# Keys and queries of every head in both row halves of the array, with odd heads scored in the upper half

## The reference

```python
x = x + attn_a(layernorm(x))   # 16 heads of 16 features, 1024 queries and 1024 keys
x = x + ffn(layernorm(x))      # ternary weights, exact gelu
x = x + attn_b(layernorm(x))   # attends over the heads of one token
x = x + ffn(layernorm(x))

def attn_a(x):                 # lora_linear: x W^T + b + 0.5 (x B^T) A^T
    q, k, v = split(lora_linear(x, Wq, ..)), split(lora_linear(x, Wk, ..)), split(lora_linear(x, Wv, ..))
    scores = einsum('bhqd,bhkd->bhqk', q, k) * SCALE
    out = einsum('bhqk,bhkd->bhqd', softmax(scores), v)
    return lora_linear(out, Wo, ..)
```

## Time and profile before

| | us |
|---|---|
| median of 3 runs | 355.96 |
| lowest and highest of them | 355.44, 357.6 |
| the profiled execution, its own time | 356.57 |
| its span from the first to the last instruction | 354.8 |
| busy in the span: PE, DVE, ACT, POOL | 328.0, 281.7, 264.0, 128.7 |
| units 2 to 5, between the first multiplications by V of neighbouring units | 20.3 each |

### The profile page before, as it was taken

One profiled execution on the slowest core, in us unless ns is written; L12 is line 12 of the kernel. 1 busy time (PEld: TensorE's weight loads), 2 busy tenths in 40 slices (PEclk: granted clock), 3 DMA queues, 4 the chain that ended last, 5 costly groups with the idle time before them and its releaser, 6 DMA issues.

```text
span 354.8 us, 5514 instructions
## 1 busy us (share of the span) xinstructions
PE 328.0 (92%) x1909; PEld 147.0 (41%) x1909; DVE 281.7 (79%) x471; ACT 264.0 (74%) x465; POOL 128.7 (36%) x133
## 2 busy tenths in 40 slices
PE   7999787999989999999999999999998957979796
PEld 2653442222222222222222234438745723647685
DVE  6456999799989999999999543517959998899774
ACT  1575114799989999999999977996479442577694
POOL 5042019999100000000005000400499976995030
PEclk9999997899999999999999999999999996999899
DMA  7936962353340000000000000000000000000011
GB/s 225 309 62 116 155 165 48 66 127 69 59 91 0 3 0 3 0 1 2 0 3 1 3 0 1 2 0 2 0 3 0 1 0 2 0 0 2 1 61 59
DMA packets 14814, 14.57 MB, mean 41 GB/s; under 512 B 4995, under 2 KB 13126, under 8 KB 14598
## 3 DMA queue, kind: packets, MB, share of 16 engines
q1 hardware_dynamic: 12358, 12.09, 14.9%
q10 hardware_dynamic: 2176, 1.64, 1.5%
q0 software_dynamic: 256, 0.52, 0.9%
HBM read 5.78 MB, written 1.05 MB: 19 GB/s over the span
## 4 chain that ended last, share of the span: by engine, by line
PE 63%; DVE 12%; SPq 10%; ACT 7%; issue 4%; DMA 2%; POOL 2%; ACTq 0%; DVEq 0%; POOLq 0%
PE ps L1417 14%; PE ps L1403 12%; SPq L535 8%; PE ps L1557 6%; PE ps L1545 6%; PE ps L1380 5%; PE ps L1332 4%; DVE mx L1095 3%; PE ps L1530 3%; PE ps L1589 2%; PE ps L1362 2%; DMA pack<-m_rows 1%; ACT ps L929 1%; PE ps L1300 1%; DVE s_wide L1202 1%
## 5 line engine op out<-in xcount | busy, mean ns | idle before, releaser
L888 ACT ACTIVATE pbuf<-ps,exp_scale 128x512 f32<-128x512 f32 x256 | 156.5, 693 | 13.7 <-PE ps L1403 10.9
L1095 DVE TENSOR_REDUCE mx<-ps 128x1 f32<-128x1024 f32 x128 | 150.4, 1219 | 11.1 <-PE ps L1380 8.1
L1403 PE MATMUL ps<-pack 64*128 64x512 f16 x256 | 87.9, 387 | 3.4 <-ACT pbuf L888 1.3
L1417 PE MATMUL ps<-pbuf,v_slot 128*32 128x512 f32 x512 | 68.8, 611 | 1.3 <-ACT parts L873 1.3
L1403 PEld LDWEIGHTS ps<-pack 64*128 64x128 f16 x256 | 23.1, 94 | 88.1 <-ACT pbuf L888 61.7
L1380 PE MATMUL ps<-pack 64*128 64x512 f16 x128 | 48.8, 385 | 4.8 <-DVE mx L1095 4.5
L1380 PE MATMUL ps<-parts,pack 64*128 64x512 f16 x128 | 49.9, 394 | 0.0
L750 POOL TENSOR_TENSOR pbuf<-wT 128x1024 f32<-128x1024 f32 (+3 forms) x32 | 48.2, 1534 | 3.5 <-ACT wT L958 3.4
L705 POOL COPY v_slot<-v_sb 128x512 f32<-128x512 f32 x8 | 4.9, 614 | 114.5 <-PE ps L1417 93.0
L681 POOL TENSOR_TENSOR rstd<-rstd,minus_half 128x2 f32<-128x2 f32 x16 | 11.4, 715 | 72.9 <-DVE rstd L1014 72.9
L1189 DVE SCALAR_TENSOR_TENSOR pack<-ps,g_unit,pack 128x512 f16<-128x512 f32 (+1 forms) x40 | 24.6, 639 | 14.1 <-ACT pack L941 14.1
(11 more groups left out here) (145 smaller groups left out, 392.7 us busy)
## 6 DMA issues: line engine op xcount, KB each, us to landing
w_nat<-in_L_ffn_w_dram SPq DMA_DIRECT2D x2, 1024.0 KB, 7.0
pack<-pack SPq DMA_DIRECT2D x3, 512.0 KB, 4.9
pack<-pbuf SPq DMA_DIRECT2D x20, 64.0 KB, 3.1
x_res<-in_L_attn_a_x_dram SPq DMA_DIRECT2D x4, 256.0 KB, 4.0
pack<-parts SPq DMA_DIRECT2D x16, 64.0 KB, 2.3
pack<-parts SPq DMA_DIRECT2D x32, 32.0 KB, 2.0
out_dram<-x_res SPq DMA_DIRECT2D x4, 256.0 KB, 2.1
w_nat<-in_L_attn_b_Wqkv_dram ACTq DMA_DIRECT2D x1, 768.0 KB, 6.7
```

Source lines behind the costliest of these rows:

```text
L888: act.activation(pbuf[:, c % 2, j, :], ps[:, b, :], ACT.Exp, scale=exp_scale[:, 0:1]).then_inc(drained[b], 1)
L1095: dve.tensor_reduce(mx[:, par, k:k + 1], ps[:, b:b + 2, :].rearrange("p b k -> p (b k)"), AX_X, ALU.max) \
L1403: pe.matmul(ps[:, b, :], k_group[0:ROWS, at, j, P * c:P * c + P].rearrange("p g t -> p (g t)"), q_rows[0:ROWS, at, qh, j, :].rearrange("p ...
L1417: ins = pe.matmul(ps[32 * j:32 * j + 32, PV_BANK, :], v_slot[:, qh, c, j, :], pbuf[:, c % 2, j, :], start=(c == 0), stop=(c == TT - 1))
```

## The change

The upper row half now holds all keys, not the far half alone, and they lie in `k_rows` and no longer in `k_far`. For group 0, one DMA more copies the near keys of its four heads up. For groups 1 to 3 the copy of the keys is 512 KB instead of 256 KB. The shift is written by two DMAs, one into each row half, and whoever waits for a shift waits for both. `score_tile` takes keys and queries of heads 1 and 3 of a group from the upper row half; heads 0 and 2 stay in the lower. The max pass reads its far keys from `k_rows`.

```diff
@@ far_keys
-            spread(eng, k_far[ROWS:2 * ROWS, h, :], K_, h, slice(HALF, T), done)
+            spread(eng, k_rows[ROWS:2 * ROWS, h, HALF:T], K_, h, slice(HALF, T), done)
@@ SP, group 0
             sp.dma_start(q_rows[ROWS:2 * ROWS, 0, 1, :, :], q_rows[0:ROWS, 0, 1, :, :]).then_inc(second_half_repeated, 16)
+            for j in range(G):
+                sp.wait_ge(head_packed[j], 32)
+            sp.dma_start(k_rows[ROWS:2 * ROWS, 0:G, 0:HALF], k_rows[0:ROWS, 0:G, 0:HALF]).then_inc(far_keys_packed, 16)
@@ SP, whole_group
-                sp.dma_start(k_far[ROWS:2 * ROWS, G * g:G * g + G, :], k_rows[0:ROWS, G * g:G * g + G, HALF:T]) \
-                    .then_inc(group_repeated[g], 16)
+                sp.dma_start(k_rows[ROWS:2 * ROWS, G * g:G * g + G, :].rearrange("p h t -> p (h t)"),
+                             k_rows[0:ROWS, G * g:G * g + G, :].rearrange("p h t -> p (h t)")).then_inc(group_repeated[g], 16)
@@ SP, land_shift
-                sp.dma_start(q_rows[SHIFT_ROWS[g // 2], g, qh, :, :].rearrange("o h t -> o (h t)"),
-                             m_rows[0:TWO * n, :]).then_inc(shift_landed, 16)
+                rows = SHIFT_ROWS[g // 2]
+                for r in (0, ROWS):
+                    sp.dma_start(q_rows[rows.start + r:rows.stop + r:rows.step, g, qh, :, :].rearrange("o h t -> o (h t)"),
+                                 m_rows[0:TWO * n, :]).then_inc(shift_landed, 16)
@@ ACT, ahead of the first exponential
-            for done in (far_keys_packed, second_half_packed):
-                act.wait_ge(done, 16 * G)
+            act.wait_ge(far_keys_packed, 16 * G + 16)
+            act.wait_ge(second_half_packed, 16 * G)
@@ PE, max_tile
-                for n, keys in ((0, k_group[0:ROWS, at, j, 0:HALF]), (1, far_group[ROWS:2 * ROWS, at, j, :])):
+                for n, keys in ((0, k_group[0:ROWS, at, j, 0:HALF]), (1, k_group[ROWS:2 * ROWS, at, j, HALF:T])):
@@ PE, score_tile
-                pe.matmul(ps[:, b, :], k_group[0:ROWS, at, j, P * c:P * c + P].rearrange("p g t -> p (g t)"),
-                          q_rows[0:ROWS, at, qh, j, :].rearrange("p g t -> p (g t)"), start=True, stop=True) \
+                r = slice(ROWS * (j % 2), ROWS * (j % 2) + ROWS)
+                pe.matmul(ps[:, b, :], k_group[r, at, j, P * c:P * c + P].rearrange("p g t -> p (g t)"),
+                          q_rows[r, at, qh, j, :].rearrange("p g t -> p (g t)"), start=True, stop=True) \
                     .then_inc(filled[b], 1)
@@ PE, ahead of unit 0 and of each next unit
-                    pe.wait_ge(far_keys_packed, 16 * G)
-                    pe.wait_ge(shift_landed, 16)
+                    pe.wait_ge(far_keys_packed, 16 * G + 16)
+                    pe.wait_ge(shift_landed, 32)
...
-                            pe.wait_ge(shift_landed, (u + 2) * 16)
+                            pe.wait_ge(shift_landed, (u + 2) * 32)
```

More of the change, by code:

```diff
@@ L313, in build @@
         last_halves = parts[:, 2048:8192].bitcast(F16).rearrange("p (m a t) -> p m a t", m=2, a=TWO + 1)
-        k_far = parts[:, 8192:16384].bitcast(F16).rearrange("p (h t) -> p h t", h=H)
         o_un = parts[:, 0:8192].bitcast(F32).rearrange("p (g t) -> p g t", g=NG)
@@ L320, in build @@
         k_group = pack[:, 0:16384].bitcast(F16).rearrange("p (g j t) -> p g j t", g=NG, j=G)
-        far_group = parts[:, 8192:16384].bitcast(F16).rearrange("p (g j t) -> p g j t", g=NG, j=G)
         g_hi = pack[:, 0:16384].bitcast(F16).rearrange("p (k f t) -> p k f t", k=KEPT, f=FC)
```

## The result

The changed kernel takes 359.31 us, the median of 22 runs (355.55 to 362.08), against 355.88 us for the kernel before in 22 runs beside it (353.6 to 357.95). The ratio is 1.0076, interval [1.0052, 1.01]: 0.8% slower, inside the 1% that the forecast calls no change. Ratios here are taken from the fast executions alone (four of the changed kernel's 22, at 361.5 us and over, count as slow), so they need not be the quotients of the medians, here 1.0096. The forecast was 357.2 us, so the time lies 2.1 us above it, 0.6 us above the forecast's own range of 356 to 358.7, and inside the wide range of 354.5 to 360.2. The profiled execution took 359.75 us, 3.2 us more than that of before; its span is 357.9 us.

A forecast was written before the change was run, and what follows sets the result against it. ACT alone bounds the steady units, PE the tail. Profiled 356.57 + 2.7 (unit 2's shift delay) - 1.5 (tail) = 357.8, by the median 357.2 us; own range 356 to 358.7, wide range 354.5 to 360.2.

The forecast's parts named there:

- a rival that I gave 0.14: Units 1 and 2: PE's longer gaps make the clock fall; at unit 2 this costs 2.8 us, giving 360.0; chance 0.14.
- Steady units, 0: Units 2 to 5: upper-half scores save PE 0.4 us per four steps, but PE waits for ACT: 0.
- Tail, -1.5: Tail, 210 to 232 us: one score pair in each of seven groups overlaps, 0.22 us each: 1.5 us less.
- gains nothing: Tail: other work takes the place of the scores, so no gain there, 358.7 us; chance 0.12.
- Group 0's near keys, 0: Extra 256 KB copy ahead of group 1: hidden by SP's 5.0 us wait for the first shift, 0; otherwise 2.0.
- The delay of unit 2's shift, +2.7: SP's queue: two second shift writes, 0.7 each, plus 1.3 for group 3's larger key copy: landing 2.7 us later.
- one unknown: Second bias load's 2.04 us on SP, amid group 2's copies: may grow or shrink by 1.3 us; taken as no change.
- group 2's extra transfer does not count a second time: At unit 2's shift: 24 small DMAs follow group 2's copy in 16 us and their issue sets the pace; nothing added.
- Unit 1's loss lies inside unit 2's: ACT's loss of about 1.9 us at unit 1 is contained in unit 2's 2.7 us delay, not added.
- a sign of being wrong: In the changed profile, a clock below 1.00 behind 83 or 105 us would speak against the forecast.
- hidden or half as large: Shift delay on SP: faster 8 KB-row copies or a shorter bias load shrink it, about 355.2 us; chance 0.15.
- PE was not the bound: Rival for units 0 to 5: PE is the bound, so some 48 rounds shrink, 19 us in all, 336; chance 0.03.

The follow-up runs named there:

- the second set: The changed kernel, unaltered, run again beside versions with idle matmuls in its gaps: 361.36 us, 1.0142 of the kernel before.

## Why the prediction came out as it did

**The change stayed under 1% in the first set, as forecast, and the mechanism was right; two terms were mis-sized, and a rival that I gave 0.14 happened in some executions.** The time missed the forecast's own range by 0.6 us, and the wide range held it because it was drawn out to the rivals. By the steps:

*Steady units, 0.* Right: 102.63 us for five units before and after, and PE's waits for ACT 15 us longer.

*Tail, -1.5.* Measured -1.2. Groups of three fell to 0.60 us and pairs to 0.39, as the step says; by the distance between starts the seven groups gained 0.21, 0.21, 0.19, 0.14, 0.22, 0.04 and 0.21 us, so most of the missing 0.3 is one pair that still took 0.56 us. The rival "gains nothing" is out.

*Group 0's near keys, 0.* Right: the first shift goes out at 54.88 (54.99 before).

*The delay of unit 2's shift, +2.7.* Measured +3.74. The two second writes cost 0.72 and 0.71 of SP's time, against 0.7 each. First issue to last landing grew from 4.39 to 5.90, 1.5, against 1.3 for the transfer alone. And the term that I entered at zero was there: the bulk copies and bias loads of group 2 took 5.23 us of SP's time instead of 4.17, **+1.06**, since the first bias load held SP 1.17 us longer. These sum to 4.0; small gains elsewhere on SP take back 0.26. This is the step that failed: "one unknown", taken at no change where the profile after shows it near its slow end of 1.3. With it falls the sentence that group 2's extra transfer does not count a second time: SP was held 1.06 us longer behind it, and the 24 small copies, whose issue is the pace, began that much later. I named a cause that fits, a queue that 256 KB more would keep full, and the key copy cut in two restored the 0.69; the reason to take the middle was only that two causes were possible. At unit 1 the forecast landing, 82.7, was met at 82.74, but the bytes sit elsewhere than I put them: 1.06 us as time of SP ahead of the issue and 0.3 behind it, not 1.3 behind it. The Trainium skill, page "DMA: Bandwidth & Descriptors", section "Anatomy of one DMA — SWDGE (gpsimd) path", gives its fit for DMAs of the gpsimd path, and these are issued by SP; an estimate by its bytes over 436 GB/s would have made the delay 2.0 us. The landings measured here don't agree with that: behind the larger key copy the query copy lands 6.2 us after its issue (median), 4.9 before, 1.3 us more for 256 KB where the estimate is 0.6.

*Unit 1's loss lies inside unit 2's.* Right in every execution read of the changed kernel: unit 2's start was set by the landing, also where ACT had lost 3.45 us at unit 1. The 0.46 us that the prediction gives as PE's wait at unit 1 is that of a weight load; PE's matmuls have no wait there before the change, and at unit 2 the weight load's wait is 1.70 us beside PE's 1.21.

*The clock.* The forecast had it at 1.00 behind both gaps, as behind the wait of 1.21 us at unit 2 before the change:

```profile
102.00:104.00 2.00, 1.71 (x13) 0.46 (x13) 1.20 (x2) 1.20 (x3) 0.00 (x0) 1.00 0.00 0
```

It fell behind unit 1's in the first profile, which the prediction had named as a sign of being wrong, and behind unit 2's in the second. At clock 1.00 the measured terms give +3.6 - 1.2 = 2.4 us, about 358.3. The median is 1 us above that, by the ratio it is 0.3 us; that the clock makes this up is not shown, since in the first profile the fall at unit 1 was swallowed. In the second set the median is 2.8 us above (in its profile 0.8 are a still later landing and about 1.0 the clock; the rest is not placed). The rival priced a fall behind unit 2's gap at 2.8 us. What ACT lost behind the landing in executions that had one was 0.9 us in the changed kernel, 0.5 with the near keys late, 1.2 with the bias loads last and 2.6 with all scores in the lower half. So the rival was right in kind for those executions, and its price an upper end.

*The other rivals.* The delay was not hidden or half as large: every part of it showed. PE was not the bound: no unit became shorter. (Two sums of the prediction are slightly off: 357.2 less 19 is 338 us and not 336, and the bounds named for the own range reach 358.9 and not 358.7.)

What stays open: how the loss at the clock divides between the two gaps, why the small copies took 15.3 or 16 us, why the changed kernel's ratio differs between the sets, and the late stage, which varied between 118.0 and 121.7 us in profiles of kernels that don't differ there.

## What to carry to other kernels

A copy that is cheap in bytes is dear where it stands ahead of something due: price it by the queue that it shares, down to the instruction that waits behind it, and first try to move the due thing ahead. Here that turned +0.8% into -0.9%, of which the profile traces 0.4% below the kernel before to unit 2's start and the tail. Where PE waits, look at the granted clock behind the wait too: its work can be slower there.

## What the runs showed of the hardware

- A DMA issue can hold SP, depending on what stands ahead in the queue: the same load took 0.69 us behind key and query copies of 768 KB and 1.86 us behind those of 1 MB; with the loads moved away, the pair of shift writes in their place took 2.93 us instead of 1.46. At unit 2 the pair stands right behind the copies and took 4.02 us behind 1 MB, 2.89 behind 768 KB.
- At clock 1.00 two score matmuls of 64 rows in different halves can end in the time of one (0.39 us for two, with one pair at 0.56); two of one half take 0.60.
- The clock behind a wait of PE at these two places, in the profiles read: 1.00 behind waits of 0.89, 1.12, 1.21, 1.32, 1.52 and 1.64 us; 0.50 to 0.54 in one of the next stretches of 2 us behind 2.07, 2.18, 2.38, 2.62, 2.96 and 3.28 us. No run set the length of a wait by itself, so this is a list and not a rule.
